# First attention layer of a two-layer kernel on Trainium2: both heads of a pair scored together, and the order of the work around the scores

## What is computed

```python
def _L0_attn_ref(x, Wq, Wk, Wv):
    ...
    H, R = (8, 64)
    b, n, d = x.shape
    Q = (x @ Wq.T).reshape(b, n, H, R)
    K = (x @ Wk.T).reshape(b, n, H, R)
    V = (x @ Wv.T).reshape(b, n, H, d)
    attn = jnp.einsum('bnhr,bmhr->bhnm', Q, K)
    attn = jax.nn.softmax(attn, axis=-1)
    out = jnp.einsum('bhnm,bmhd->bnd', attn, V)
    return out
...
x = x + _layernorm(_L0_attn_ref(_layernorm(x, axis=-1), L0_attn_Wq, L0_attn_Wk, L0_attn_Wv), axis=-1)
```

## Time and profile before

| what | us |
|---|---|
| median of 3 runs | 2117.53 |
| lowest and highest run | 2064.26, 2120.01 |
| span of the profiled execution | 2081.0 |
| TensorE busy in it | 1778.6 (85%) |
| VectorE busy | 1214.5 (58%) |
| ScalarE busy | 927.3 (45%) |
| mean granted TensorE clock | 0.858 |

### The profile page before, as it was taken

One profiled execution on the slowest core, in us unless ns is written; L12 is line 12 of the kernel. 1 busy time (PEld: TensorE's weight loads), 2 busy tenths in 40 slices (PEclk: granted clock), 3 DMA queues, 4 the chain that ended last, 5 costly groups with the idle time before them and its releaser, 6 DMA issues.

```text
span 2081.0 us, 31701 instructions
## 1 busy us (share of the span) xinstructions
PE 1778.6 (85%) x10724; PEld 954.1 (46%) x10724; DVE 1214.5 (58%) x2711; ACT 927.3 (45%) x2162; POOL 375.6 (18%) x208
## 2 busy tenths in 40 slices
PE   7999999999999879964999989989947886778766
PEld 4454444444544443332544545445524554245543
DVE  6554645546555546673665556546577764467744
ACT  2333423334333223322766657657525564255632
POOL 0000000000000002331000000000017873078820
PEclk8899988999999979985876668678778998889978
DMA  4000000000000000012000000000010000000000
GB/s 106 0 1 0 0 0 0 0 0 0 0 0 0 0 0 0 0 56 86 18 14 14 22 23 11 12 23 2 2 46 1 0 1 1 1 1 0 1 1 20
DMA packets 25961, 24.10 MB, mean 12 GB/s; under 512 B 4834, under 2 KB 19500, under 8 KB 25804
## 3 DMA queue, kind: packets, MB, share of 16 engines
q1 hardware_dynamic: 25836, 22.52, 3.6%
HBM read 18.32 MB, written 4.19 MB: 11 GB/s over the span
## 4 chain that ended last, share of the span: by engine, by line
PE 66%; POOL 12%; DVE 10%; issue 8%; ACT 2%; SPq 1%; DMA 1%; POOLq 0%; DVEq 0%; ACTq 0%
PE ps L568 12%; PE ps L591 11%; PE ps L796 7%; PE ps L578 7%; PE ps L740 5%; PE ps L766 5%; POOL ss L1862 4%; POOL probsT L1873 3%; PE ps L758 2%; DVE arena L1291 2%; PE ps L700 2%; POOL q_st L1860 2%; PE ps L804 2%; PE ps L694 1%; PE ps L541 1%
## 5 line engine op out<-in xcount | busy, mean ns | idle before, releaser
L1291 DVE CUSTOM_DVE_ANT_0 arena<-ps,arena 128x128 f32<-128x128 f32 (+7 forms) x258 | 194.2, 753 | 210.8 <-PE ps L740 161.1
L568 PE MATMUL ps<-k_st,q_st 64*128 64x512 f32 x512 | 269.0, 650 | 6.7 <-ACT probs L1557 6.7
L1115 DVE TENSOR_REDUCE negmax<-ps 128x1 f32<-128x1024 f32 x128 | 156.7, 1224 | 194.8 <-PE ps L568 194.8
L591 PE MATMUL ps<-probsT,v_st 128*128 128x512 f32 x512 | 238.7, 599 | 0.0
L1654 ACT ACTIVATE probs<-arena,negmax 128x128 f32<-128x128 f32 (+7 forms) x258 | 199.8, 775 | 57.9 <-DVE negmax L1294 54.9
L1563 ACT COPY probsT<-ps 128x512 f32<-128x512 f32 x128 | 74.9, 585 | 307.3 <-PE ps L578 307.3
L796 PE MATMUL ps<-ident,probs 128*128 128x128 f32 x832 | 190.6, 355 | 7.6 <-ACT probsT L1680 3.2
L1680 ACT COPY probsT<-ps 128x512 f32<-128x512 f32 (+3 forms) x256 | 127.2, 497 | 132.9 <-PE ps L796 132.2
L1557 ACT ACTIVATE probs<-ps,negmax 128x1024 f32<-128x1024 f32 x128 | 142.6, 1114 | 51.9 <-DVE negmax L1115 50.9
L578 PEld LDWEIGHTS ps<-ident,probs 128*128 128x128 f32 x1024 | 118.0, 147 | 100.8 <-issue 76.1
L796 PEld LDWEIGHTS ps<-ident,probs 128*128 128x128 f32 x832 | 113.9, 175 | 101.0 <-issue 87.3
(11 more groups left out here) (243 smaller groups left out, 2969.7 us busy)
## 6 DMA issues: line engine op xcount, KB each, us to landing
c_parts<-arena SPq DMA_DIRECT2D x4, 768.0 KB, 4.3
yT<-c_parts SPq DMA_DIRECT2D x64, 48.0 KB
arena<-in_L_ffn_w_dram SPq DMA_DIRECT2D x3, 512.0 KB
work<-in_L_ffn_wqkv_dram SPq DMA_DIRECT2D x1, 1536.0 KB
q_st<-c_parts SPq DMA_DIRECT2D x32, 48.0 KB
k_st<-c_parts SPq DMA_DIRECT2D x32, 48.0 KB
x_sb<-in_L_attn_x_dram SPq DMA_DIRECT2D x2, 512.0 KB, 4.5
yT<-c_parts SPq DMA_DIRECT2D x32, 32.0 KB
```

The source lines that it names most:

```text
L568: ins = pe.matmul(ps[:, 2 * (u % 2) + n, :], q_st[r:r + R0, qt * P:(qt + 1) * P], k_st[r:r + R0, n * CH:(n + 1) * CH], start=True, stop=True)
L591: ins = pe.matmul(ps[:, 6 + qc, :], v_st[:, kt, head * P:(head + 1) * P], probsT[:, c % 2, kt, :], start=(head == 0 and kt == 0), stop=(he ...
L1115: dve.tensor_reduce(negmax[:, u:u + 1], s2, AX_X, ALU.max, negate=True)\
L1291: dve.tensor_tensor_reduce(c_sb[:, u % 2, 0:w], s2, c_T[:, j, SEQ - w:SEQ], 1.0, -3.0e38, ALU.add, ALU.max, cmax[:, u:u + 1]).then_inc(s_c ...
```

## The change

The two heads of the pair now go together. Step i (of 8) handles units 2i and 2i+1, which are query tile i of head 0 and of head 1. `scores(i)` issues four matmuls that alternate between the heads, into all four score banks, and waits until both exps of the step before are done. Scores stand between the transposes of unit 2i-2 and those of unit 2i-1, and value matmuls come in fours behind each of the two. A chunk of the value matmuls is 256 queries of one head (`HC`), seen through `a_pT`, another view of the same `probsT`; a head's chunk takes eight matmuls of 256 columns. Values have a second buffer (`a_v[1]`, in `v_nat`), so the value projection of the next block stands ahead of the last eight value matmuls. VectorE does both row maxima, then the older copies and scalings; ScalarE does both exps between its two copies.

```diff
+HC = 256
...
+        a_pT = probsT[:, :, :, :].rearrange("p a k c -> p (a k c)")\
+            .rearrange("p (s n k c) -> p s n k c", s=2, n=2, k=QT)
...
+        a_v = [v_st[:, :, :], v_nat[:, :, :].rearrange("p (k n) c -> p k (n c)", n=2)]
...
-                    def scores(u):
-                        r, qt = R0 * (u // QT), u % QT
-                        if u == 0:
+                    def scores(i):
+
+                        if i == 0:
                             pe.wait_ge(s_a_q, m + 1)
                             pe.wait_ge(s_a_k, m + 1)
                             pe.wait_ge(s_a_v0, m + 1)
-                        elif u == 1:
                             pe.wait_ge(s_a_v1, m + 1)
                         else:
-                            pe.wait_ge(s_a_exp, n0 + u - 1)
+                            pe.wait_ge(s_a_exp, n0 + 2 * i)
                         for n in range(2):
-                            ins = pe.matmul(ps[:, 2 * (u % 2) + n, :], q_st[r:r + R0, qt * P:(qt + 1) * P],
-                                            k_st[r:r + R0, n * CH:(n + 1) * CH], start=True, stop=True)
-                        ins.then_inc(s_a_scores, 1)
+                            for head in range(2):
+                                r = R0 * head
+                                ins = pe.matmul(ps[:, 2 * head + n, :], q_st[r:r + R0, i * P:(i + 1) * P],
+                                                k_st[r:r + R0, n * CH:(n + 1) * CH], start=True, stop=True)
+                                if n == 1:
+                                    ins.then_inc(s_a_scores, 1)
...
                         if k0 == 0:
-                            pe.wait_ge(s_a_evA, n0 + 4 * c + 5)
-                            pe.wait_ge(s_a_evB, n0 + 4 * c + 5)
+                            pe.wait_ge(s_a_evA, n0 + 4 * c + head + 4)
+                            pe.wait_ge(s_a_evB, n0 + 4 * c + head + 4)
...
                         for kt in range(k0, k1):
-                            ins = pe.matmul(ps[:, 6 + qc, :], v_st[:, kt, head * P:(head + 1) * P],
-                                            probsT[:, c % 2, kt, :], start=(head == 0 and kt == 0),
+                            ins = pe.matmul(ps[:, 6 + c // 2, (c % 2) * HC:(c % 2 + 1) * HC],
+                                            a_v[b][:, kt, head * P:(head + 1) * P],
+                                            a_pT[:, c % 2, head, kt, :], start=(head == 0 and kt == 0),
...
-                    for u in range(NU):
-                        scores(u)
-                        if u >= 2:
-                            turn(u - 2)
-                        if u >= 6:
-                            c, k = (u - 6) // 4, (u - 6) % 4
-                            weigh(c, 2 * k, 2 * k + 2)
+                    for i in range(QT):
+                        if i >= 1:
+                            turn(2 * i - 2)
+                        if i >= 3:
+                            weigh((i - 3) // 2, (i - 3) % 2, 0, 4)
+                        scores(i)
+                        if i >= 1:
+                            turn(2 * i - 1)
+                        if i >= 3:
+                            weigh((i - 3) // 2, (i - 3) % 2, 4, 8)
...
                     a_proj_q(nb)
                     turn(NU - 2)
-                    weigh(2, 4, 6)
+                    weigh(2, 1, 0, 6)
+                    turn(NU - 1)
+                    weigh(2, 1, 6, 8)
                     pe.wait_ge(s_a_exp, n0 + NU)
                     a_proj_k(nb)
-                    turn(NU - 1)
-                    weigh(2, 6, 8)
-                    weigh(3, 0, 8)
+                    weigh(3, 0, 0, 8)
                     a_proj_v(nb, m + 2)
+                    weigh(3, 1, 0, 8)
...
-                    for u in range(NU):
+                    for i in range(QT):
+                        u = 2 * i
                         rowmax(u)
-                        if u >= 1:
-                            rrecip(u - 1)
-                        if u >= 2:
+                        rowmax(u + 1)
+                        if i >= 1:
                             copy_out(u - 2)
-                    rrecip(NU - 1)
+                        rrecip(u)
+                        if i >= 1:
+                            copy_out(u - 1)
+                        rrecip(u + 1)
                     copy_out(NU - 2)
-                    a_evac_k(m + 2)
                     copy_out(NU - 1)
                     add_out(0)
+                    a_evac_k(m + 2)
+                    a_evac_v(m + 2, 1 - b)
                     add_out(1)
-                    a_evac_v(m + 2)
...
-                    for u in range(NU):
-                        if u >= 2:
+                    for i in range(QT):
+                        u = 2 * i
+                        if i >= 1:
                             copy_out(u - 2)
                         soft(u)
+                        soft(u + 1)
+                        if i >= 1:
+                            copy_out(u - 1)
+                    a_evac_q(m + 2)
                     copy_out(NU - 2)
-                    a_evac_q(m + 2)
                     copy_out(NU - 1)
-                    a_evac_v(m + 2)
+                    a_evac_v(m + 2, 1 - b)
```

More of the change, by code:

```diff
@@ L580, in turn, with weigh @@
                             ins.then_inc(s_a_trans, 1)
-                    def weigh(c, k0, k1):
-                        head, qc = c // 2, c % 2
+                    def weigh(c, head, k0, k1):
                         if k0 == 0:
-                            pe.wait_ge(s_a_evA, n0 + 4 * c + 5)
-                            pe.wait_ge(s_a_evB, n0 + 4 * c + 5)
-                            if head == 0:
+                            pe.wait_ge(s_a_evA, n0 + 4 * c + head + 4)
+                            pe.wait_ge(s_a_evB, n0 + 4 * c + head + 4)
+                            if c == 0 and head == 0:
                                 pe.wait_ge(s_a_oadd, 2 * m + 1)
                         for kt in range(k0, k1):
-                            ins = pe.matmul(ps[:, 6 + qc, :], v_st[:, kt, head * P:(head + 1) * P],
-                                            probsT[:, c % 2, kt, :], start=(head == 0 and kt == 0),
+                            ins = pe.matmul(ps[:, 6 + c // 2, (c % 2) * HC:(c % 2 + 1) * HC],
+                                            a_v[b][:, kt, head * P:(head + 1) * P],
+                                            a_pT[:, c % 2, head, kt, :], start=(head == 0 and kt == 0),
                                             stop=(head == 1 and kt == QT - 1), skip_group_check=True)
-                        if head == 1 and k1 == QT:
+                        if c % 2 == 1 and head == 1 and k1 == QT:
                             ins.then_inc(s_a_pv, 1)
-                    for u in range(NU):
-                        scores(u)
-                        if u >= 2:
-                            turn(u - 2)
-                        if u >= 6:
-                            c, k = (u - 6) // 4, (u - 6) % 4
-                            weigh(c, 2 * k, 2 * k + 2)
+                    for i in range(QT):
[8 more added lines that the diff above has]
+                            weigh((i - 3) // 2, (i - 3) % 2, 4, 8)
                     nb = 1 - b
@@ L1097, in a_evac_k, with a_evac_v @@
                 dve.tensor_copy(k_st[:, :].rearrange("p (n c) -> p n c", n=2), ps[:, 2:4, :]).then_inc(s_a_k, 1)
-            def a_evac_v(m):
+            def a_evac_v(m, b):
                 dve.wait_ge(s_a_projv1, m)
-                dve.tensor_copy(v_st[:, 4:8, :].rearrange("p (n k) c -> p n (k c)", n=2),
+                dve.tensor_copy(a_v[b][:, 4:8, :].rearrange("p (n k) c -> p n (k c)", n=2),
                                 ps[:, 2:4, :]).then_inc(s_a_v1, 1)
             a_evac_k(1)
-            a_evac_v(1)
+            a_evac_v(1, 0)
             dve.wait_ge(s_a_ozero, 1)
@@ L1537, in a_evac_q, with a_evac_v @@
                 act.copy(q_st[:, :].rearrange("p (n c) -> p n c", n=2), ps[:, 0:2, :]).then_inc(s_a_q, 1)
-            def a_evac_v(m):
+            def a_evac_v(m, b):
                 act.wait_ge(s_a_projv0, m)
-                act.copy(v_st[:, 0:4, :].rearrange("p (n k) c -> p n (k c)", n=2), ps[:, 0:2, :]).then_inc(s_a_v0, 1)
+                act.copy(a_v[b][:, 0:4, :].rearrange("p (n k) c -> p n (k c)", n=2), ps[:, 0:2, :])\
+                   .then_inc(s_a_v0, 1)
             act.activation(sd[:, 0:1], eps_c[:, 0:1], ACT.Exp)
             a_evac_q(1)
-            a_evac_v(1)
+            a_evac_v(1, 0)
             with act.Fori(0, PAIRS) as p:
@@ L1561, in copy_out @@
                         act.wait_ge(s_a_trans, 2 * (n0 + u) + 1)
-                        c, q = u // 4, (u % 4) * P
-                        act.copy(probsT[:, c % 2, 0:4, q:q + P],
+                        c, q = u // 4, (u // 2 % 2) * P
+                        act.copy(a_pT[:, c % 2, u % 2, 0:4, q:q + P],
```

(12 more changed lines are left out.)

4 lines of the change are left out of this document (2 added, 2 removed).

## The result

| | before | changed |
|---|---|---|
| median of six runs each, us | 2089.7 | 2136.16 |
| lowest and highest | 2064.26, 2120.01 | 2125.71, 2185.23 |
| profiled execution: its time, span | -, 2081.0 | 2125.71, 2123.9 |

A forecast was written before the change was run, and what follows sets the result against it. TensorE was taken to bound the changed stage. Profiled span 2081 + 56 (full clock) - 29 (long low stretches gone) + 51 (short ones) = 2159, with about 16 carried over: 2175 us, range 2130 to 2250.

The forecast's parts named there:

- The wait: TensorE, second half of the odd unit's transposes: waits 2.7 us for VectorE's copy, 7 times a block.
- Behind the first scores: Start of each block: TensorE waits 3.7 us before the transposes of unit 0, which need its scaling.
- The overlap: Both heads' scores on different row halves: eight passes in the time of four, 1.72 us saved a pair, 13.8 a block.
- Four slots, not five: Score matmuls of a pair: four pass slots kept; five, by strict program order, would add 0.43 us a pair, 27 us.
- The value buffer and the 256-column matmuls at nothing: Block end and value matmuls: no time either way; if the cover of the evacuations failed, 1.2 us a block.
- Short low stretches: TensorE's clock behind the new waits: 30 of 64 bring 3 to 3.5 us at half clock, 51 us, bounds 0 to 109.
- The two long ones: Long half-clock stretches in the profile of the kernel before: two, 29 us, expected to go.
- Full clock +56: First attention's eight blocks: 24.4 us of waits added, 17.4 removed, net +7.0 us a block.
- 16 were carried over: Step from profiled span to median: about 16 us added for what does not belong to this stage, giving 2175.
- the forecast's own case: Whole kernel: waits as worked out, 15 to 45 short clock falls, 2145 to 2205 us; chance 0.54.
- Not slower: the clock pays it back: Rival, TensorE's clock: fewer than about 15 short falls remain, 2108 us; chance 0.16.
- Nearly every wait: Rival: the clock falls at nearly all 64 waits, 1.7 us each, 2233 us or more; chance 0.19.

The follow-up runs named there:

- e4_head_by_head: Changed kernel with head 0's two score matmuls issued first, then head 1's two, instead of alternating; 2150.1 us, one run.
- e2_copy_late: Changed kernel with VectorE's copy of unit 2i-2 moved behind the reciprocal and scaling of unit 2i; 2265.32 us, one run.
- e3_one_row_half: Changed kernel with both heads' score matmuls on rows 0 to 63, head 1's own scores left out of the result; 2268.54 us.
- e9_first_one_half: Changed kernel with each step's scores first in TensorE's order, and both heads' score matmuls on rows 0 to 63; 2117.13 us, one run.

## Why the prediction was right, and where its sizes were off

- **Direction and mechanism: right.** Faster scores, given back as a wait for VectorE's copy. Start of the copy 4.30 us into the step, measured 4.29; second half of the transposes at 5.04, measured 5.03; step 9.98, measured 9.95.
- **The wait** was put at 2.7 us, and the record has 2.45; the difference is the tail that the record counts as busy. 56 of them, as forecast. Behind the first scores 3.7, recorded 3.53; 16 of 0.9, recorded 0.57 on average (0.63 at full clock), with the same tail.
- **The overlap: right.** Four slots, not five: 1.99 us for eight passes. The Trainium skill ("TensorE: Matmul & The Clock Gate", Part 3, what overlaps and what doesn't) lets matmuls start in program order only; e4_head_by_head, issued head by head, also took 2.00 us, so the measurement decides against that rule for matmuls on different row halves.
- **The value buffer and the 256-column matmuls at nothing: right** as far as it goes. Eight passes of 256 columns are recorded with 1.89 us, like four of 512 in the earlier trace rows.
- **The clock: right in kind, mis-sized in number.** Short low stretches came; the forecast took 30 of them and 51 us. There are 18, 65 us long together, and half of that is a loss of 32 us. The two long ones (29 us) went, as forecast. Full clock +56, clock +32 - 29: +59, and the loop measured +60 like for like. The forecast had said itself that no row tells the number; 30 was a guess, and too high.
- **Where the 39 us between 2175 and 2136 went.** The sum for the span was 2159, and the profiled span is 2123.9, 35 less. Of these, 19 are the low stretches that did not come, and 17 are the part of the kernel that was not changed: its spread between executions, which had no term in the sum. The other 4 us are the step from the span to the median: 16 were carried over, and it measured 12 (2136.16 - 2123.9). That the 16 came so near is luck. They do not follow from the prediction's own reasoning, in which 36.5 us less two falls of 14.7 leave 7, and the 36.5 rested on a median of three runs; with six the kernel before has 2089.7, 8.7 above its span.
- **How narrowly it held.** 2136 is 6 us inside the lower end of the range, outside the 2145 to 2205 of the forecast's own case, and below the border of 2160 at which "slower by over 2%" began, which had a chance of 0.70. Only the lower median of the kernel before makes 2136 a change of 2.2%; the forecast was 2.7% above 2117.5. The chances do not add up as worded either: three quarters of 0.54, and 0.27, are 0.68.
- **Rivals.** "Not slower: the clock pays it back" is not confirmed, as 18 short falls are more than the 15 at which it was to decide, and their loss (32) cancels the pay-back (29). It was the nearest rival, though: the profiled span lies 16 us from its 2108 and 35 from the 2159 of the sum. "Nearly every wait" fell: 18 of 64. It was nearer in e2_copy_late: waits of 3.6 us, a mean clock of 0.82 in the loop, and twice the loss of the waits alone.

## What to carry to other kernels

When work is taken off the engine that bounds, walk the other engines' queues from the moment that the shortened step starts: an older copy that stands behind new work which waits for this very step is not late on average, it is late every time. Before moving the copy, ask whether the bound engine can be given its other work first: here one call moved in TensorE's order turned 2.6% slower into 4% faster (ratios 1.026 and 0.958 to the kernel before), where moving the copy only brought the kernel level. And compare the changed stage between profiles before whole times: here the untouched part alone moved by up to 47 us. Busy shares showed none of it; VectorE was busy 58% of the span before and 57% after.

## What the runs showed of the hardware that was not expected

- Two matmuls in different row halves of the array need not alternate in the program to overlap: eight passes took 1.99 us in alternation and 2.00 us head by head.
- A busier TensorE did not have the higher clock. e3_one_row_half kept TensorE busier than the changed kernel (763 of 866 us, against 563 of 739) and had a mean clock of 0.84, against 0.96. Low stretches of 10 us and more came only where the scores used 64 rows of the array at a time: the kernel before (two of 31 us, one of them that of the earlier trace rows), e3_one_row_half (eight of 24 to 31 us) and e9_first_one_half (eight of 10 to 31). In the loops of the others none was longer than about 7 us. Why is not shown: the edit to one row half also changes how long the scores take and how long TensorE waits.
- The blocks of the changed kernel are of one length, to a few hundredths of a us, once they settle (92.13 to 92.16 us from projection to projection, six times), with the low stretches at the same places in each.
